# Turning a graph network's count tables by DMA in layer 2 instead of layer 4

## The reference

```python
x = _layernorm(x + L0(x, edge_index, edge_type_64, ...))   # layer 1: segment sum of messages with a relation vector
x = _layernorm(x + L1(x, src, dst, ...))                   # layer 2: attention, softmax over edges of a node
x = _layernorm(x + L2(x, edge_index, edge_type_2, ...))    # layer 3: two kinds of edges
x = _layernorm(x + L3(x, edge_index, ...))                 # layer 4: segment sum by src of normed h[dst]

def _L3_gnn_ref(x, edge_index, W, b):
    h = jnp.einsum('nd,od->no', x, W) + b
    ...
    messages = norm[:, None] * h[col]
    out = jax.ops.segment_sum(messages, row, num_segments=n)
    return out
```

## Time and profile before

| | us |
|---|---|
| median of 3 runs (4124.19 to 4128.95) | 4126.3 |
| the profiled execution, its time | 4132.2 |
| the profiled execution, its span from first to last instruction | 4130.5 |
| last store of the tables issued in layer 1 | 1717.6 |
| first SP instruction of the second layer's block | 1788.20 |
| last work of the second layer's block starts, first load of layer 3 | 2814.80, 2820.28 |
| first transposing load of layer 4, last one | 3645.07, 4110.1 |

### The profile page before, as it was taken

How to read it: one execution, slowest core, us unless ns; L and a number is a source line. 1 busy time by engine, 2 the same in 40 slices (tenths; PEclk the granted TensorE clock), 3 DMA queues, 4 the chain that set the end, 5 groups by cost and what they waited for, 6 DMA issues and landing times. The chain is left out here.

```text
span 4130.5 us, 90438 instructions
## 1 busy us (share of the span) xinstructions
PE 3511.6 (85%) x36615; PEld 2901.3 (70%) x36740; DVE 3204.4 (78%) x3960; ACT 2337.2 (57%) x5142; POOL 391.8 (9%) x336
## 2 busy tenths in 40 slices
PE   2666777776999999869999999996999999967776
PEld 1555666664666666569999999995888888845554
DVE  7999999998777777589999999996666666723233
ACT  4998999996555555423333333334666666634343
POOL 3003211122111111100000000001000000000000
PEclk9999999997999999879999999998999999989999
DMA  3000000001322222200000000002333333268988
GB/s 107 2 2 2 2 2 2 2 2 37 114 110 110 111 111 110 77 2 2 2 2 2 2 2 2 2 2 85 99 101 101 99 101 103 86 116 170 168 170 172
DMA packets 423099, 257.10 MB, mean 62 GB/s; under 512 B 329994, under 2 KB 419863, under 8 KB 422548
## 3 DMA queue, kind: packets, MB, share of 16 engines
q1 hardware_dynamic: 422196, 248.79, 22.7%
q10 hardware_dynamic: 480, 2.40, 0.2%
HBM read 86.93 MB, written 85.49 MB: 42 GB/s over the span
## 5 line engine op out<-in xcount | busy, mean ns | idle before, releaser
L97 DVE TENSOR_TENSOR both_hot<-iota_own,recs 128x1792 bf16<-128x1792 bf16 (+1 forms) x686 | 754.4, 1107 | 231.5 <-PE rR L1466 121.9
L1830 ACT ACTIVATE gC<-qC 128x896 f32<-128x896 f32 x343 | 314.7, 918 | 647.6 <-PE qC L1850 647.6
L1862 PE MATMUL qO<-A,gC 128*128 128x132 f32 x4802 | 615.3, 280 | 0.0
L1862 PEld LDWEIGHTS qO<-A,gC 128*128 128x128 f32 x4802 | 566.6, 190 | 0.0
L1474 PE MATMUL rO<-sl_f,terms 128*128 128x384 bf16 (+1 forms) x1934 | 476.4, 355 | 3.7 <-DVE A L1242 2.2
L2174 ACT ACTIVATE some_r<-rC 128x512 fp32r<-128x512 f32 (+1 forms) x686 | 336.4, 543 | 252.6 <-PE rC L2204 252.1
L628 PE MATMUL pV<-VO,PM 128*128 128x70 bf16 (+4 forms) x6524 | 259.8, 199 | 236.2 <-ACT PM L484 159.7
L1432 ACT ACTIVATE sl_f<-rC 128x896 bf16<-128x896 f32 x343 | 313.8, 915 | 255.2 <-PE rC L1454 254.4
L2454 PE MATMUL tO<-tables_r,Xr 128*128 128x448 f32 x1372 | 357.6, 392 | 116.5 <-ACT tables_r L2322 80.1
L91 DVE TENSOR_TENSOR PM<-iota_b,place 128x2944 bf16<-128x2944 bf16 (+2 forms) x226 | 410.4, 1816 | 30.8 <-ACT place L464 30.4
L1466 PE MATMUL rR<-rel_hot,both_hot 128*128 128x65 bf16 x2450 | 410.9, 194 | 25.5 <-DVE A L1242 12.2
(11 more groups left out here) (298 smaller groups left out, 6225.4 us busy)
## 6 DMA issues: line engine op xcount, KB each, us to landing
tables<-sl_f SPq DMA_DIRECT2D x343, 224.0 KB, 1.9
sl_f<-tables SPq DMA_DIRECT2D x343, 224.0 KB, 2.5
sl_f<-tables SPq DMA_TRANSPOSE x343, 3.7
edges<-terms SPq DMA_DIRECT2D x1, 3528.0 KB, 11.2
B<-in_x SPq DMA_DIRECT2D x1, 2744.0 KB
out<-B SPq DMA_DIRECT2D x7, 392.0 KB
terms<-in_edge_type ACTq DMA_DIRECT2D x2, 686.0 KB
terms<-in_edge_weight ACTq DMA_DIRECT2D x1, 686.0 KB
```

What stands on the lines that cost most here:

```text
L97: return v.tensor_tensor(o.rearrange("p n k (a b) -> p (n k) a b", b=2), iota_own[:, 0:w].rearrange("p (a b) -> p a b", b=2).unsqueeze(1). ...
L1862: mm = pe.matmul(pO[i % SUMS][:, 0:XW], Cs[:, U % 2, j, :], A[:, a, :], start=a == 0, stop=a == NT - 1)
```

## The change

A second DRAM array `turned_d` (`turned_tables`) holds the 343 units already transposed. In the block of layer 2, SP reads each unit from `tab_d` with the transposing DMA that layer 4 used, into one of three new SBUF buffers `turning`, and stores it from there to `turned_d` in plain rows. Layer 4 loads units from `turned_d` with plain DMAs; all else there stays. The other lines adapt the semaphore counts.

```diff
+    turned_d = nc.dram_tensor("turned_tables", (UNITS, P, G7 * P), BF16, kind="Internal").ap()
...
+        TURNS = 3
+        TURNED = [STORED[b] + (32 * len(range(b, UNITS, TURNS)) if b < TURNS else 0) for b in range(RING)]
...
+                turning = sb("turning1", [P, TURNS, G7 * P], BF16, c)
...
                         sp.dma_start(vec[:, :], vector_of("scale0").rearrange("(a n) -> a n", a=1).broadcast_to([P, P])).then_inc(s_load, 16)
+                        for U in range(UNITS + TURNS - 1):
+                            if U < UNITS:
+                                m, b = U // NT, U % NT
+                                first = b // G7 * NT + m * G7
+                                if U >= TURNS:
+                                    sp.wait_ge(s_tab[U % TURNS], STORED[U % TURNS] + 32 * (U // TURNS))
+                                sp.dma_start_transpose(turning[:, U % TURNS, :], tab_d[first:first + G7, :, b % G7 * P:(b % G7 + 1) * P].rearrange("u p d -> (u p) d")).then_inc(s_tab[U % TURNS], 16)
+                            done = U - (TURNS - 1)
+                            if done >= 0:
+                                sp.wait_ge(s_tab[done % TURNS], STORED[done % TURNS] + 32 * (done // TURNS) + 16)
+                                sp.dma_start(turned_d[done], turning[:, done % TURNS, :]).then_inc(s_tab[done % TURNS], 16)
+                        for b in range(TURNS):
+                            sp.wait_ge(s_tab[b], TURNED[b])
...
-                    return 2 * STORED[U % RING] + 16 * (U // RING + 1)
+                    return TURNED[U % RING] + STORED[U % RING] + 16 * (U // RING + 1)
...
-                            m, b = unit(U)
-                            first = b // G7 * NT + m * G7
-                            table = tab_d[first:first + G7, :, b % G7 * P:(b % G7 + 1) * P].rearrange("u p d -> (u p) d")
-                            sp.dma_start_transpose(kept[U % RING], table).then_inc(s_tab[U % RING], 16)
+                            sp.dma_start(kept[U % RING], turned_d[U]).then_inc(s_tab[U % RING], 16)
```

More of the change, by code:

```diff
@@ L1973, in convert @@
                                 v.wait_ge(s_all, U - 1)
-                            v.wait_ge(s_tab[U % RING], STORED[U % RING] + 16 * (U // RING + 1))
+                            v.wait_ge(s_tab[U % RING], TURNED[U % RING] + 16 * (U // RING + 1))
                             v.tensor_copy(all_r[:, U % 2, :], kept[U % RING]).then_inc(s_kept[0], 1)
@@ L2119, in convert @@
                                 act.wait_ge(s_all, U - 1)
-                            act.wait_ge(s_tab[U % RING], STORED[U % RING] + 16 * (U // RING + 1))
+                            act.wait_ge(s_tab[U % RING], TURNED[U % RING] + 16 * (U // RING + 1))
                             act.activation(all_r[:, U % 2, :], kept[U % RING], ACT.Copy).then_inc(s_kept[1], 1)
```

## The result

The changed kernel takes 4349.5 us (median of 4 runs, 4345.0 to 4350.3) against 4127.6 us before (median of 4 runs). The ratio is 1.0537, 95% interval 1.0522 to 1.0553: slower by 222 us. The forecast was 4386 us, 6.3% slower.

What follows compares the result with a forecast made beforehand. Only layer 4 was held short of data, by transposing loads at 1.36 us a unit. Layer 2's loop +341 and layer 4 -81 give +260 us: 4392 on the profiled execution, 4386 us at the median, range 4150 to 4580.

Steps and rivals of the forecast that it cites:

- What bounds layer 4: Layer 4: transposing loads pace it at 1.36 us a unit; plain loads cut 464.7 to 385 us, gaining 81 us in all.
- the conversion buffer's round of 2.18 us: Layer 4, when fed: conversion 0.96, four matmuls 1.10, hand-over about 0.1 us; two units a round, 1.09 us each.
- The 12 us for the changes of group: Layer 4: estimated one lost round at each of six group changes, added to 373 us to give 385 us.
- Which wait is in series in layer 2: Layer 2, SP's turning loop: each round holds one transposing issue and the whole landing of the store just issued.
- How long a round is: Layer 2's turning loop: 4.0 us a round, within bounds of 3.25 and 5.6 us, for 340 rounds.
- +341: Layer 2: the turning loop ends at 3156.6, 341 us after the other engines, which stand at the barrier.
- 3.8 to 4.1: Layer 2's loop: store landing in us from the transposing issue's start, 3.2 to 3.5 for the load plus 0.63.
- the 3.24 of break-even: Layer 2's loop: a round of 3.24 us would leave the whole time unchanged, counting layer 4's 81 us gain.
- A store that does not queue: Layer 2 rival: the store does not wait behind the load; round 3.25 us, +86 - 81 = +5, 4131 us; chance 0.07.
- A short issue on an empty queue: Layer 2 rival: transposing issue costs 0.33 us, round 2.3 us, loop wholly hidden, 4045 us; chance 0.05.
- Full serialisation: Layer 2 rival: store begins only once the load ahead has landed; round 5.6 us, +885 - 81 = +804, 4930 us; chance 0.05.
- plain rows bring nothing: Layer 4 rival: something else paces it at 1.36 us a unit, so no gain; 4126 + 341 = 4467 us; chance 0.05.

## Why the prediction was right

- **What bounds layer 4.** The forecast read the pace of 1.36 us a unit as that of the transposing load, and with plain rows the conversion buffer's round of 2.18 us as next. Both held: 385 us forecast, 385.4 measured, and the run without turning gives 84 us for the whole, 81 forecast. The third conversion buffer shows that it was this round. The 12 us for the changes of group, an estimate in that sum, no run measures by itself. One part of the reading was off: the issue of 1.29 us is not wholly the form's own. With waits between, it took 1152 ns, so some 0.14 us came from issuing back to back.
- **Which wait is in series in layer 2.** This step carried the sign, and moving the store by one unit shows it directly: 4349 against 4045 us with the same buffers and the same transfers.
- **How long a round is.** 4.0 us forecast, 3.89 measured. The 340 rounds took 1324 us in place of 1360, and these 36 us are what made +305 of +341, and nearly all of the distance from 4386 to 4349. The terms inside: 1.33 us of issue was 1.20 with the gap, and 2.67 us of landing behind a load was 2.4 as a median and 2.7 as a mean. The mean needs the long rounds, which the forecast did not have; a round without a fetch, 3.61 us, is below its 3.8 to 4.1, in part because the load ahead landed in 3.1 us and not in 3.2 to 3.5. Two errors stood against each other, so it was luck that the 4.0 came so near; the sign did not hang on it, since 3.61 is above the 3.24 of break-even too.
- **The Trainium skill**, "DMA: Bandwidth & Descriptors", section "Queues, rings and completion order": a semaphore comes only after that DMA engine's earlier writes. The trace agrees as far as it goes: the store landed 1.20 + 2.4 = 3.6 us after the issue of the load ahead, which itself landed in 3.1.
- **The rivals.** A store that does not queue (4131 us, a round of 3.25) fell with the 1.9, 2.4 and 2.9 us of landing. A short issue on an empty queue (4045 us) fell with a minimum of 1151 ns. Full serialisation (4930 us) fell with 3.89 us. That plain rows bring nothing (4467 us) fell with the 84 us.

## What to carry to other kernels

A ring of n buffers between a load and a store has n - 1 steps of slack to share out between "the load has landed" and "the store has landed". A loop that stores as late as the ring allows leaves none for the store, and each round then contains its whole landing, with five buffers as with three. Before work is moved under another stage, compare rounds times latency with that stage's length, and not bytes with bandwidth: here 1.87 us of DMA time a unit (0.47 x 1031 / 259) would have fitted into 3.0 us, and 3.9 us of latency did not.

## What the runs showed of the hardware

- A 224 KB store to DRAM, waited for, lands 1.9 us after its issue begins with nothing ahead, 2.4 us when a transposing load of the same size was issued 1.2 us before, and 2.9 us when a plain one was issued just before.
- The issue of a transposing load of 128 x 896 bf16 holds SP's queue for 1152 ns with waits between and 1287 ns back to back, a plain one 320 ns. The issue of the store behind a transposing load showed 578 ns, where alone it took 319.
- Turning all 343 units at 2.03 us each beside layer 2 left its end where it was, and the kernel's time at that of the run without turning (4045.3 and 4044.5 us).
- In the loop that waits for its store, a round with an instruction fetch under way took 4.30 us in the mean against 3.61 without, and 115 transfers of the same 16 KB in packets of 512 bytes changed nothing (258 stores in the window against 259).
